# Gated cross attention with a quantised feed-forward part: row sums, attended values, norms and weight transposes move between engines

## The reference

```python
# x (4,1024,256), ctx (4,154,256); B=4 batches
hc = layernorm(x)                                   # "h"
w1, w2, w3 = w_sim[:d], w_sim[d:2*d], w_sim[2*d:]
Sim = (hc @ w1)[:, :, None] + (ctx @ w2)[:, None, :] + einsum('bid,bjd->bij', hc * w3, ctx) + b_sim
A = softmax(Sim, axis=2)
hq_hat = einsum('bij,bjd->bid', A, ctx)             # attended values
Batt = softmax(max(Sim, axis=2), axis=1)            # one weight per row of x
hc_bar = einsum('bi,bid->bd', Batt, hc)             # one vector per batch
feats = concat([hc, hq_hat, hc * hq_hat, hc * hc_bar], -1)
x = x + tanh(g_xattn) * (feats @ W_qv + b_qv)       # W_qv (1024,256): blocks W0, W1, W2, W3
x = x + tanh(g_ffn) * ffn(layernorm(x))             # 4-bit weights, 16-bit activations, 256 -> 768 -> 256
```

## Time and profile before

| | |
|---|---|
| median of 3 runs | 488.28 us (487.01 to 489.61) |
| profiled execution | 486.99 us, span 485.2 us |
| TensorE matmuls | 461.5 us, 95% of the span |
| VectorE | 344.0 us, 71% |
| ScalarE | 266.7 us, 55% |
| GpSimd | 63.1 us, 13% |
| granted TensorE clock, mean | 0.993 |

### The profile page before, as it was taken

The page is one execution under the profiler, slowest core; times in us unless marked ns, Lnnn a source line. Parts: engine busy times, 40 slices in busy tenths (PEclk is TensorE's granted clock), DMA queues, the critical chain, the costliest instruction groups (busy, mean ns, idle before and its releaser), DMA issues.

```text
span 485.2 us, 6854 instructions
## 1 busy us (share of the span) xinstructions
PE 461.5 (95%) x2528; PEld 304.6 (63%) x2528; DVE 344.0 (71%) x649; ACT 266.7 (55%) x325; POOL 63.1 (13%) x61
## 2 busy tenths in 40 slices
PE   4899999998999997998999999999999999799997
PEld 3787884986578846783444444444444444588886
DVE  6455483859264935687644378999998888898874
ACT  3795142624241300426633459999567777888760
POOL 1111111213110311310000003343200000000000
PEclk9999999999899998999999999999999999999999
DMA  8930000200020002002000000000000000234442
GB/s 236 327 119 1 0 2 0 88 0 1 1 88 0 1 0 86 2 0 88 0 0 0 0 1 0 0 1 0 0 1 1 0 0 0 88 111 151 135 142 72
DMA packets 20673, 21.15 MB, mean 44 GB/s; under 512 B 825, under 2 KB 20392, under 8 KB 20648
## 3 DMA queue, kind: packets, MB, share of 16 engines
q1 hardware_dynamic: 20628, 20.82, 13.5%
q10 hardware_dynamic: 20, 0.00, 0.0%
HBM read 12.43 MB, written 8.39 MB: 43 GB/s over the span
## 4 chain that ended last, share of the span: by engine, by line
PE 68%; issue 15%; DVE 13%; ACT 2%; POOL 1%; DMA 1%; ACTq 0%; POOLq 0%; DVEq 0%
PE ps L676 17%; PE ps L711 11%; PE ps L681 9%; PE ps L527 4%; PE ps L506 4%; PE ps L531 4%; PE ps L523 4%; PE ps L569 3%; PE ps L486 3%; PE ps L472 1%; PE ps L495 1%; DVE st L1066 1%; PE ps L462 1%; DVE xa L1062 1%; DVE yb L1079 1%
## 5 line engine op out<-in xcount | busy, mean ns | idle before, releaser
L676 PE MATMUL ps<-xh,wuh 128*128 128x512 f16 x192 | 72.8, 379 | 0.1
L676 PE MATMUL ps<-xh,wul 128*128 128x512 f16 x192 | 72.8, 379 | 0.0
L681 PE MATMUL ps<-xl,wuh 128*128 128x512 f16 x192 | 57.1, 379 | 0.0
L1300 DVE TENSOR_REDUCE cols<-hid x10 | 22.9, 2286 | 24.7 <-ACT hid L891 24.7
L711 PE MATMUL ps<-wdl,oh 128*128 128x256 f16 x168 | 37.4, 273 | 0.0
L711 PE MATMUL ps<-wdh,oh 128*128 128x256 f16 x168 | 37.4, 273 | 0.0
L676 PE MATMUL ps<-xh,wgh 128*128 128x512 f16 x96 | 36.4, 379 | 0.7 <-DVE xh L1288 0.7
L676 PE MATMUL ps<-xh,wgl 128*128 128x512 f16 x96 | 36.4, 379 | 0.0
L527 PE MATMUL ps<-wv,prT 128*128 128x256 f32 x128 | 35.9, 396 | 0.0
L523 PE MATMUL ps<-cw,aT 77*128 77x256 f32 x128 | 34.7, 385 | 0.9 <-ACT cols L840 0.9
L783 ACT ACTIVATE hT<-ps 128x512 f32<-128x512 f32 x16 | 9.5, 591 | 46.6 <-PE ps L472 46.6
(11 more groups left out here) (211 smaller groups left out, 953.5 us busy)
## 6 DMA issues: line engine op xcount, KB each, us to landing
x_scratch<-xa SPq DMA_DIRECT2D x4, 1024.0 KB, 4.4
xo<-x_scratch SPq DMA_DIRECT2D x16, 256.0 KB, 2.7
out_dram<-xo SPq DMA_DIRECT2D x15, 256.0 KB, 2.1
xa<-in_x SPq DMA_DIRECT2D x3, 1024.0 KB, 12.6
xa<-in_x SPq DMA_DIRECT2D x4, 256.0 KB, 4.3
wv<-in_L_xattn_W_qv SPq DMA_DIRECT2D x1, 1024.0 KB, 8.6
wr<-in_L_ffn_w_gate SPq DMA_DIRECT2D x1, 768.0 KB, 9.5
wr<-in_L_ffn_w_up SPq DMA_DIRECT2D x1, 768.0 KB, 10.9
```

Source lines behind the costliest of these rows:

```text
L676: pe.matmul(ps[hf][:, q, :], w_[:, d, ds(k * P, P)], xh[:, d, n], start=d == 0 and w_ is wh, stop=False)
L681: mm = pe.matmul(ps[hf][:, q, :], wh[:, d, ds(k * P, P)], xl[:, d, n], start=False, stop=d == KD - 1)
L1300: dve.tensor_reduce(gmx[:, ds(k * 2 + hf, 1)], unit(hid, k, hf), AX.X, ALU.max, apply_absolute_value=True).then_inc(gm_done, 1)
```

## The change

1. `row_sum`, `row_copy` and the tile `hrow` go. Instead ScalarE (tiles 0 to 3) and GpSimd (tiles 4 to 7) scale the eight tiles of h by `eb` in place (`row_weigh`, step with s = 1), GpSimd adds the tiles up to one (`row_add`, step with s = 2), and `batch_cols`, now in the step with s = 3, multiplies this tile by a column of ones.
2. `context_w`, `context_wv` and the tile `cw` go. The attended values are copied out of PSUM by ScalarE (`attended`, into `hqT`), and `project` multiplies them by W1 (`wv[:, KD + d]`). VectorE's `attended` reads `hqT` instead of PSUM. The bias b_qv, times tanh(g), is added to x by GpSimd (`bias_x`), two units at a time in the steps with s = 3 and s = 0.
3. `norm_x` is on VectorE, in one step from mean and 1/std; `row_shift` goes.
4. The first projection of a batch is split: `project_first` (W1 and W2, no `we` needed) at the start of the step with s = 3, and `project_rest` (with `we`) at its end.
5. The weight transposes are nine slots, spread over steps 17 to 22, instead of three blocks in steps 19 to 21.

```diff
+        TURNS = [(1, 0), (1, 1), (1, 2), (0, 0), (0, 1), (0, 2), (2, 0), (2, 1), (2, 2)]
+        TURN_AT = {17: (0,), 18: (1,), 19: (2, 3), 20: (4, 5), 21: (6, 7), 22: (8,)}
...
+            def row_weigh(b):                                   # GpSimd
+                par = b % 2
+                pool.wait_ge(eb_rdy, b + 1)
+                for t in range(TB // 2, TB):
+                    i_ = pool.tensor_scalar(h[:, par, t, :], h[:, par, t, :], eb[:, t:t + 1], 1.0, ALU.mult, ALU.mult)
+                i_.then_inc(hp_rdy, 1)
+                pool.wait_ge(hp_rdy, b + 1)
+                pool.tensor_tensor(h[:, par, 4:6, :], h[:, par, 4:6, :], h[:, par, 6:8, :], ALU.add).then_inc(hsum_rdy, 1)
+
+            def row_add(b):
+                pool.wait_ge(ha_rdy, b + 1)
+                pool.tensor_tensor(h[:, par, 0:2, :], h[:, par, 0:2, :], h[:, par, 2:4, :], ALU.add).then_inc(hsum_rdy, 1)
+                pool.wait_ge(hsum_rdy, 3 * b + 2)
+                pool.tensor_tensor(h[:, par, 0:2, :], h[:, par, 0:2, :], h[:, par, 4:6, :], ALU.add).then_inc(hsum_rdy, 1)
+                pool.wait_ge(hsum_rdy, 3 * b + 3)
+                pool.tensor_tensor(h[:, par, 0, :], h[:, par, 0, :], h[:, par, 1, :], ALU.add).then_inc(hs_rdy, 1)
+
+            def bias_x(n):
+                pool.wait_ge(h_rdy, n + 1)
+                x_ = xa[:, 2 * n:2 * n + 2, :]
+                pool.tensor_tensor(x_, x_, txb[:].unsqueeze(1).broadcast_to([P, 2, D]), ALU.add).then_inc(xb_rdy, 1)
...
+                if s == 3 and 4 <= m < N + 4:                   # GpSimd's step
+                    for n in range(2):
+                        bias_x(m - 5 + n)
                 if LAG <= m < L + LAG:
                     y_std(m - LAG)
+                if s == 1 and 1 <= b <= B:
+                    row_weigh(b - 1)
+                if s == 2 and 1 <= b <= B:
+                    row_add(b - 1)
                 if 1 <= m and m + 3 < N:
                     row_std(m + 3)
+                if s == 0 and 4 <= m < N + 4:
+                    for n in range(2):
+                        bias_x(m - 4 + n)
...
                 if LAG <= m and not late:                       # TensorE's step
-                    project(m - LAG, b - 1 if s == 2 and 1 <= b <= B else None)
+                    project(m - LAG)
+                if LAG <= m and late:
+                    project_first(b - 1)
...
-                if s == 2 and 1 < b <= B:
+                if s == 3 and 1 <= b <= B:
                     batch_cols(b - 1)
                 if 3 <= m <= N + 2:
                     attend(m - 3)
...
-                if s == 0 and 1 <= b < B:
-                    context_w(b)
                 if LAG <= m and late:
-                    project(m - LAG)
-                if N + 3 <= m < N + 6:
-                    turn_w(m - N - 3)
+                    project_rest(b - 1)
+                for i in TURN_AT.get(m, ()):
+                    turn_w(i)
...
+            def attended(n):                                    # ScalarE
+                act.wait_ge(hq_ps, n + 1)
+                ge(act, f_ps, n - 2 * NP + 1)
+                act.activation(hqT[:, par, :, s * PT:(s + 1) * PT], hq_bank.rearrange("p (d n) -> p d n", d=KD),
+                               ACT.Copy).then_inc(hqT_rdy, 1)
...
+            def row_weigh(b):
+                act.wait_ge(eb_rdy, b + 1)
+                for t in range(TB // 2):
+                    a_ = act.activation(h[:, b % 2, t, :], h[:, b % 2, t, :], ACT.Copy, scale=eb[:, t:t + 1])
+                a_.then_inc(ha_rdy, 1)
...
                     normed(m - 1)                               # ScalarE's step
...
+                if 3 <= m <= N + 2:
+                    attended(m - 3)
+                if s == 1 and 1 <= b <= B:
+                    row_weigh(b - 1)
...
+            def norm_x(n):                                      # VectorE
+                dve.wait_ge(rstd_rdy, n + 1)
+                ge(dve, hc_ps, b - 1)
+                for t in range(2 * s, 2 * s + 2):
+                    i_ = dve.tensor_scalar(h[:, par, t, :], xa[:, b * TB + t, :], mv[:, par, t, 0:1], rstd[:, c:c + 1],
+                                           ALU.subtract, ALU.mult)
...
-                dve.wait_ge(hq_ps, n + 1)
+                dve.wait_ge(hqT_rdy, n + 1)
                 dve.wait_ge(hT_rdy, n + 1)
...
+                if s == 3 and 1 <= b <= B:                      # VectorE's step
+                    summary(b - 1)
                 if 3 <= m <= N + 2:
                     attended(m - 3)
+                if s == 3 and 3 < m and m + 1 < N:
+                    norm_x(m + 1)
                 if LAG <= m and late:
                     residual(m - LAG)
                     norm_x1(m - LAG)
...
+                for i in TURN_AT.get(m, ()):
+                    weight_part(i)
+            for i in TURN_AT[N + LAG - 1]:
+                weight_part(i)
             last_y()
```

## The result

The changed kernel takes 476.06 us (median of 4 runs, 474.58 to 476.78), the kernel before on the same chip 488.94 us (4 runs, 487.01 to 490.62). The ratio is 0.9732, with a 95% interval of 0.9699 to 0.9766. It is faster, by 2.7% and not by the 4.8% that I forecast: 465 us was 11 us too low, and 476.06 lies one microsecond above my range. The profiled execution took 476.41 us, with a span of 474.6 and a mean granted clock of 0.968 (0.993 before).

The account below looks back on a forecast made before the run. TensorE bounds the stretch ahead of the feed-forward part; in steps 8 to 15 the bound passes to VectorE. Savings 3 + 11 + 11 - 3.2 = 21.8 us from 486.99 give 465 us, range 460 to 470, with two rivals 455 to 475.

Parts of the forecast that it names:

- my second rival: All 9 us a batch of GpSimd holds on VectorE, and idle time lowers TensorE's clock: 475 us, chance 0.18.
- Row sums, W1, split projection off TensorE: Steps 8 to 15: with the removed work gone, TensorE's batch falls from 46.97 to 39.5 us.
- VectorE becomes the bound at "45 to 46" a batch: Steps 8 to 15: VectorE, 38.8 us a batch plus GpSimd's holds, becomes the bound at 45 to 46 us.
- TensorE's lead of about one half step (4) is used up first: Steps 8 to 15: VectorE needs 91 us, but TensorE's lead of 4 is spent first, so 87; saved 11.
- What TensorE waits for is `we` in steps 11 and 15, 2 to 5 us each: At `project_rest` in steps 11 and 15, TensorE would idle 2 to 5 us each for `we`.
- TensorE idle under 5 us in steps 8 to 15: Sign that the forecast is wrong and TensorE stays the bound in steps 8 to 15.
- the first rival: TensorE stays the bound, holds fall into VectorE's waits, steps 8 to 15 save 18.4: 458 us, chance 0.17.
- Nothing of `norm_x` or first statistics is left on VectorE here, so TensorE is the bound again: Step 16 to the last projection: TensorE bounds again, 12.4 us go, less 1.3 idle for `summary`; saved 11.
- GpSimd's prices: New GpSimd work: 1.05 us per 512-wide addition, 0.6 per 256-wide one, 0.3 per scaling; 36.6 us in all.
- The wait of 1.45 us for `hqT` ahead of `prT`: In every step VectorE waits about 1.45 us between its reciprocal and `prT` for ScalarE's copy of the attended values.
- Start to step 8: TensorE loses 3.5 + 1.7 and about 1 us; VectorE pacing steps 3 to 6 gives back about 3; saved 3.
- Tail: After the last projection: VectorE begins the last rows 2.5 us later, behind the ninth weight slot's subtraction; lost 3.2.

Follow-up runs that it names:

- e3: The changed kernel without GpSimd's new work: no bias added to x, no GpSimd scalings or additions for the row sums; 458.57 us.
- e4: The changed kernel with matmuls that nothing reads filling TensorE's idle places in steps 11, 15, 18 and 19; 473.06 us.
- e1: The changed kernel with VectorE's `attended`, which forms `prT`, moved behind the statistics in each step; 470.01 us.
- e2: The changed kernel with the nine weight slots in steps 17, 19, 20 and 21, none in 18 or 22; 474.69 us.
- e10: The changed kernel with bias on TensorE, `prT` behind the statistics, weight slots moved, and row sums as 16 one-column matmuls a batch; 473.25 us.
- e16: e10 with 14 of the 16 one-column matmuls a batch widened to 128 columns, result unread; 466.05 us.
- e12: The changed kernel with the bias moved from GpSimd to float16 matmuls into the projection's bank on TensorE; 464.31 us.
- e13: e12 plus GpSimd additions that nothing reads, at the places of the old `bias_x`; 472.89 us.
- e14: e12 plus GpSimd writes of a constant that nothing reads, at the places of the old `bias_x`; 465.04 us.

## Why the forecast was 11 us too low

The steps that failed are two terms of the sum: that behind step 16 VectorE and GpSimd hold nothing up (item 5, 5.9 us), and the lead of TensorE (item 3, 3.6 us). The holds and the low clock that I gave to my second rival were there in every batch.

1. *Row sums, W1, split projection off TensorE: right.* With GpSimd's new work away (e3) a batch is 39.2 and 39.8 us; I had worked out 39.5 for TensorE alone.
2. *VectorE becomes the bound at "45 to 46" a batch: right in size, by two errors.* Measured 44.5 and 44.4. My own sum for VectorE without the new holds was 38.8 + 3 = 41.8, yet e3 runs a batch in 39.2 to 39.8, so that sum was at least 2 us too long; and the new work of GpSimd, taken at 3 to 4 a batch, costs 4.6 to 5.4, the lower clock included. The hold of `prT`, which I left out of the sum and bounded by 8 us, is 13.5 - 11.0 = 2.5 us against e3; that of `we`, which I did not name, is 3.2.
3. *"TensorE's lead of about one half step (4) is used up first": wrong, 3.6 us.* In step 7 `project_rest` already waits 1.07 us for `we` (48.32). The stage began without a lead and took 90.55 and not 87. That VectorE paces steps 3 to 6, which I had written myself, would explain it; no run tests that by itself.
4. *"What TensorE waits for is `we` in steps 11 and 15, 2 to 5 us each": wrong.* At 92.86 and 137.29 `project_rest` starts with no idle time ahead. TensorE's idle time in these stages is 4.2 us, ahead of `turn_a` and `batch_cols` (0.56, 1.20 and 2.39), and the rest of what VectorE costs it is spent in slower matmuls. In e4, where the matmuls of step 15 are faster again, a wait of 2.22 us for `we` appears (135.52). So "TensorE idle under 5 us in steps 8 to 15", my sign for the first rival, came true although the first rival did not: at the lower clock TensorE looks busy.
5. *"Nothing of `norm_x` or first statistics is left on VectorE here, so TensorE is the bound again": wrong, 5.9 us, the largest miss.* I took holds and clock at nothing behind step 16. GpSimd's new work costs 6.4 us in this batch (40.14 against 33.70). The 0.92 and 2.97 us of idle time of the earlier trace rows went, as forecast, but 2.55 + 2.13 us of new idle time came (168.64, 177.43), and the clock is 0.84 to 0.92 in the windows from 160 to 190. In e4, where the clock is 1.00 from 140 to 200, the batch still takes 39.48, so that most of this is not the clock.
6. *GpSimd's prices: too low.* A 512-wide addition takes 1.27 to 1.33 (1.05 taken), a 256-wide one 0.73 to 0.94 (0.6), a scaling 0.55 (0.3): 48.8 us in all against 36.6.
7. *The wait of 1.45 us for `hqT` ahead of `prT`: right in kind.* 13 waits, 15.9 us, 1.2 each. e1 shows that an order of VectorE takes it away and gives 6.0 us. By itself it bounds nothing: e3 has 14.8 us of the same waits, and its TensorE is idle for only 1.2 of 79.0 us in steps 8 to 15.
8. *Start to step 8: right as a sum,* 3.7 against 3; its terms were not measured one by one. *Tail: right in kind,* 4.6 against 3.2. Its rows after, against the earlier trace rows:

```profile
200.34 0.60 PE L592 MATMUL ps<-ident,yb 128*128 128x128 f32 x4
...
201.47 0.59 ACT L894 ACTIVATE wdh<-ps 128x512 f16<-128x512 f32 x1
202.09 0.69 DVE L1215 TENSOR_TENSOR wdl<-ps,wdh 128x512 f16<-128x512 f32 x1 [2.56 <-ACT wdh L894]
202.70 0.48 DVE L1133 SCALAR_TENSOR_TENSOR xa<-ps,cols,xa 128x256 f32<-128x256 f32 x1
...
205.18 0.44 PE L603 MATMUL ps<-ident,yb 128*128 128x128 f32 x2 [1.64 <-DVE yb L1144]
```

   The last rows begin 2.36 us behind the projections, as worked out (2.5). The rest goes mostly with the transposes behind them and the lower clock (0.79 from 200 to 210, where the tail before had 1.00). e2, without the slot, has the old tail and a clock of 1.00 in it.
9. *Feed-forward part: 1.1 us longer.* TensorE has 1.1 us of idle time there for `gq`. No run was made for it; it stays open.

Together 3.6 + 5.9 + 1.4 + 1.1 - 0.7 = 11.3, which is the 11.2 of the table within rounding. What happened is my second rival ("the holds are worse, and the idle time lowers the clock"), with its time of 475; "all 9 us a batch" of holds is more than was there (GpSimd's new work costs 4.6 to 6.4 a batch, clock included), so the nearness of 475 is in part luck. I gave it 0.18 against 0.6, mainly because "VectorE has waits in which GpSimd can run". They did not help: the additions follow `y_std` directly and so run just when VectorE's next scaling is due (126.34 to 129.77 and 127.70 above).

## What to carry to other kernels

Price work that goes to GpSimd not by whether it fits into that engine's idle time, but by which reads of VectorE it meets; here 48.8 us of it on an idle engine cost 17.5 us of the kernel, and the part that went to TensorE instead, as one narrow-format matmul a half unit, cost nothing that could be measured. Before counting on a lead or slack, look whether the engine already waits where the stage begins. Where an instruction waits on a copy that another engine has just begun, put work that is ready between them.

## What the runs showed of the hardware

- TensorE's granted clock fell without any idle time: 32 records of one-column matmuls (4.47 us), then 0.50 for 8 us with TensorE busy 4.00 of 4.00 (e10, profiled run); with 128 columns and the same weights it stayed at 1.00 (e16). The page "TensorE: Matmul & The Clock Gate" of the Trainium skill, section "What's actually happening", ties the clock to how busy the engine has been; in e10 the clock fell while the profile showed TensorE busy all the time.
- Sixteen one-column float32 matmuls in a row took 4.33 us, 0.27 each, at a clock of 0.79 (e10). At full clock a single one among wider ones took 0.14 to 0.15, and one of 128 columns 0.23 (e16, starts of rows).
- GpSimd writing a constant did not hold VectorE's two-input operations (`prT` 0.69 inside 3.00 us of writes, `we` 0.48 on average, as in e12); GpSimd's additions did (`prT` 1.76 in the changed kernel, `we` 0.73 on average in e13 and 0.88 in the changed kernel). Single scalings were lengthened a little by the writes too (0.98 us for two at 89.80, e14).
- A float16 matmul of 256 columns is 0.11 us between float32 ones of 0.43.
